# Opening of a graph layer kernel: rows of x and ids loaded first, weights behind the table rows, and part of the normalisation moved to GpSimd and VectorE

## The reference

```
gnn: e   = edge_attr @ W_edge + b_edge
     agg = segment_sum(relu(xn[src] + e), dst)
     h   = relu(((1 + eps) * xn + agg) @ W1 + b1) @ W2 + b2
     relu(batchnorm(h) * gamma + beta)
mix: linear attention over the nodes, 8 heads, weights Wq, Wkv, Wproj
ffn: softmax router, 8 experts, top 2 of them, two-layer MLP with gelu
```

## Time and profile before

| What | Value |
|---|---|
| Runs | 1181.65, 1177.09, 1177.69 us; median 1177.69 |
| Span of the profiled execution, first to last instruction | 1050.8 us |
| The profiled execution's own time | not given apart from its span; the median lies 126.9 us above the span |
| PE busy | 964.7 us (92%) |
| VectorE busy | 671.7 us (64%) |
| GpSimd busy | 555.1 us (53%) |
| ScalarE busy | 513.5 us (49%) |
| DMA | 198.30 MB, mean 189 GB/s |

### The profile page before, as it was taken

One profiled execution on the slowest core, in us unless ns is written; L12 is line 12 of the kernel. 1 busy time (PEld: TensorE's weight loads), 2 busy tenths in 40 slices (PEclk: granted clock), 3 DMA queues, 4 the chain that ended last, 5 costly groups with the idle time before them and its releaser, 6 DMA issues.

```text
span 1050.8 us, 17977 instructions
## 1 busy us (share of the span) xinstructions
PE 964.7 (92%) x5112; PEld 810.3 (77%) x5113; DVE 671.7 (64%) x1274; ACT 513.5 (49%) x1036; POOL 555.1 (53%) x627
## 2 busy tenths in 40 slices
PE   5898999999999999999998961799999999999994
PEld 4677888888888888877775860778888888888884
DVE  5455565656655565578886778666666666666663
ACT  3644555555454545455554566444444444444442
POOL 3277777777777777777760040224253353444442
PEclk8899999999999999999998986899999999999998
DMA  9667788788888878998762028412545636635321
GB/s 246 197 154 237 255 267 253 250 268 266 260 254 262 269 247 267 278 313 270 239 202 86 26 89 316 181 26 40 204 90 174 220 50 213 192 73 160 98 38 21
DMA packets 85472, 198.30 MB, mean 189 GB/s; under 512 B 19785, under 2 KB 37139, under 8 KB 84378
## 3 DMA queue, kind: packets, MB, share of 16 engines
q1 hardware_dynamic: 55926, 131.60, 36.1%
q0 software_dynamic: 28752, 64.45, 25.5%
q10 hardware_dynamic: 724, 1.42, 0.5%
HBM read 147.86 MB, written 49.97 MB: 188 GB/s over the span
## 4 chain that ended last, share of the span: by engine, by line
POOL 29%; PE 29%; DMA 19%; issue 13%; DVE 7%; ACT 2%; POOLq 1%; SPq 0%; DVEq 0%; ACTq 0%
POOL work L758 29%; DMA out<-work,rowc 11%; PE banks L1141 6%; PE banks L1166 4%; DMA work<-token_table,tokc 4%; PE banks L470 3%; PE banks L446 3%; PE banks L1168 2%; PE banks L969 2%; PE banks L1054 2%; PE banks L1151 2%; DMA work<-in_edge_attr 1%; PE banks L1042 1%; DMA wts<-in_src 1%; DVE st L1776 1%
## 5 line engine op out<-in xcount | busy, mean ns | idle before, releaser
L758 POOL DMA_INDIRECT work<-node_table,srcT x391 | 379.5, 971 | 157.0 <-issue 117.6
L470 PE MATMUL banks<-work 128*128 128x256 f32 x780 | 179.1, 379 | 1.1 <-issue 1.1
L446 PE MATMUL banks<-w_edge,eaT 128*128 128x256 f32 x780 | 179.3, 380 | 0.0
L470 PEld LDWEIGHTS banks<-work 128*128 128x128 f32 x780 | 148.0, 190 | 21.8 <-issue 1.8
L446 PEld LDWEIGHTS banks<-w_edge,eaT 128*128 128x128 f32 x780 | 143.4, 191 | 16.8
L1166 PE MATMUL banks<-wsplit,hidT_hi 128*128 x416 | 153.3, 408 | 2.1 <-DVE hidT_lo L1908 2.1
L529 DVE TENSOR_TENSOR work<-banks,work 128x512 f32<-128x512 f32 x195 | 126.8, 682 | 26.1 <-DMA work<-node_table,srcT 15.2
L1141 PE MATMUL banks<-wsplit,xeT_hi 128*128 x416 | 134.3, 404 | 2.8 <-DVE xeT_lo L1915 2.8
L483 ACT COPY wts<-banks 128x256 f32<-128x256 f32 x66 | 24.6, 372 | 228.8 <-PE banks L470 227.8
L811 POOL DMA_INDIRECT out<-work,rowc x52 | 83.4, 1605 | 82.2 <-ACT work L1441 45.6
L1168 PE MATMUL banks<-wsplit,hidT_lo 128*128 x416 | 116.8, 281 | 0.0
(11 more groups left out here) (263 smaller groups left out, 1555.2 us busy)
## 6 DMA issues: line engine op xcount, KB each, us to landing
wsplit<-split_table SPq DMA_DIRECT2D x8, 4096.0 KB, 15.3
work<-in_edge_attr SPq DMA_DIRECT2D x65, 384.0 KB, 4.6
wts<-in_L_ffn_W SPq DMA_DIRECT2D x64, 256.0 KB, 4.9
split_table<-raw_hi SPq DMA_DIRECT2D x64, 256.0 KB, 3.0
split_table<-raw_lo SPq DMA_DIRECT2D x64, 256.0 KB, 4.3
work<-node_table,srcT POOLq DMA_INDIRECT x391, 4.2
xs<-in_x SPq DMA_DIRECT2D x8, 560.0 KB
wts<-in_L_ffn_b SPq DMA_DIRECT2D x8, 512.0 KB, 4.0
```

Source lines behind the costliest of these rows:

```text
L446: last = nc.tensor.matmul(b[:, k * DIM:(k + 1) * DIM], eaT[:, u, 2 * q + k], w_edge[:], start=True, stop=True)
L470: last = nc.tensor.matmul(bank[5][:, 0:DIM], onehot[:, u, j], msg[:, u, j], start=(j == 0), stop=(j == GT - 1))
L758: pool.indirect_dma_start(out=xg[n % NB][0:rows, j], out_offset=None, in_=node_table, in_offset=bass.IndirectOffsetOnAxis(ap=srcT[0:rows, ...
```

## The change

Chunks 1 and 2 of x are now first on ScalarE's queue, ahead of the bias row, the router's weights, `eps` and `w_edge`; chunks 3 and 4 follow the ids on SP. The other weights are loaded behind the stores of the table rows. The rounds are (0), (1), (2), (3 and 4). The seven small steps from moments to variance run on POOL. The bias additions of chunks 0, 1, 2 run on POOL, those of 4 and 3 on VectorE, which also normalises chunk 4 itself. Every chunk has its own place in `table_stage`. The clearing of `hT` moves behind POOL's additions. The destination ids (`rel`) are worked out after the bias additions, and their transposes come after the routing. PE's transposes of x alternate between banks 0 to 2 and 3 to 5. The mixing weights are transposed in group 0 of the edge phase (`turn_weights`), in two halves with ScalarE's copies between them, and VectorE's first one-hot waits for them (`wT_ready` 2), since it shares their place in SBUF.

```diff
-STAGES = 4
-LEAD = ((0,), (1, 2), (3, 4))
+ROUNDS = ((0, 1), (1, 2), (2, 3), (3, 5))
+BY_POOL = 3
...
@@ sync @@
-            load_x(2)
+            load_x(3)
             load_x(4)
-            weights = [
...
-            for s, d in weights:
-                sp.dma_start(s, d).then_inc(weights_in, 16)
             load_edges(sp, 0, 0, 0, True)
-            load_edges(sp, 1, 1, 1, True)
...
+            for c, ready, n in ((0, rows_pool, 1), (1, rows_pool, 2), (4, rows_dve, 1), (2, rows_pool, 3), (3, rows_dve, 2)):
+                sp.wait_ge(ready, n)
+                for d, s in node_rows(node_table, table_stage[c], c):
+                    sp.dma_start(d, s).then_inc(rows_stored, 16)
+            sp.dma_start(w_natural[:, 2:6], a["L0_mix_Wkv"].rearrange("(r p) c -> p r c", p=P)).then_inc(weights_in, 16)
+            load_edges(sp, 1, 1, 1, True)
...
+            sp.wait_ge(rows_stored, 32 * CHUNKS)
@@ gpsimd @@
+            def moments(r):
+                lo, hi = ROUNDS[r]
+                pool.wait_ge(stats_ready, r + 1)
...
+                step(nc.gpsimd.tensor_tensor(L[:, 0], v[:, 1], v[:, 4], ALU.subtract))
+                step(nc.gpsimd.tensor_tensor(L[:, 1], v[:, 1], v[:, 4], ALU.add))
+                step(nc.gpsimd.tensor_tensor(L[:, 0], L[:, 0], L[:, 0], ALU.mult))
+                step(nc.gpsimd.tensor_tensor(L[:, 2], v[:, 2], v[:, 5], ALU.add))
+                step(nc.gpsimd.tensor_scalar(L[:, 2], L[:, 2], 1.0 / DIM, LN_EPS, ALU.mult, ALU.add))
+                step(nc.gpsimd.tensor_scalar(L[:, 0], L[:, 0], 0.25, None, ALU.mult))
+                step(nc.gpsimd.tensor_tensor(L[:, 2], L[:, 2], L[:, 0], ALU.add))
+                pool.sem_inc(var_ready, 1)
...
+            for r in range(3):
+                moments(r)
+            add_bias(0)
+            moments(3)
+            for c in range(1, BY_POOL):
+                add_bias(c)
             nc.gpsimd.memset(hT[:], 0.0).then_inc(h_zero, 1)
@@ tensor @@
+                if c == 1:
+                    pe.wait_ge(wc_ready, 1)
+                    pe.wait_ge(tables_ready, 2)
...
+            def turn_weights():
+                pe.wait_ge(weights_in, WEIGHT_DMAS * 16)
+                pe.wait_ge(miss_known, 1)
...
+                last.then_inc(wT_ready, 1)
+                pe.wait_ge(wT_copied, 2)
...
+                last.then_inc(wT_ready, 1)
+                pe.wait_ge(wT_copied, 4)
@@ vector @@
+            stats_of(0).then_inc(stats_ready, 1)
+            scale_of(0)
+            stats_of(1).then_inc(stats_ready, 1)
+            stats_of(2).then_inc(stats_ready, 1)
+            dve.wait_ge(ids_in, 64)
+            nc.vector.tensor_copy(src_f, src_i).then_inc(rel_ready, 1)
+            scale_of(1)
+            stats_of(3)
+            scale_of(2)
+            stats_of(4).then_inc(stats_ready, 1)
...
+            scale_of(3)
+            normalise_x(4)
+            dve.wait_ge(small_in, SMALL_DMAS * 16)
+            add_bias(4)
+            add_bias(3)
             dve.wait_ge(wc_sum, 1)
```

More of the change, by code:

```diff
@@ L134, in build @@
         onehot = view(work, 7680, 2, GT, P)
-        table_stage = view(work, 1536, STAGES * CHUNK_TILES, DIM).rearrange("p (u t) d -> p u t d", u=STAGES)
+        table_stage = [view(t, o, CHUNK_TILES, DIM) for t, o in ((work, 1536), (work, 2816), (work, 4096), (work, 5376), (wts, 0))]
         w_natural = view(work, 7168, 8, DIM)
@@ L283, in build @@
         xn_ready = sem("xn_ready")
-        rows_ready = sem("rows_ready")
-        rows_stored = [sem(f"rows_stored{i}") for i in range(STAGES)]
+        xn_last = sem("xn_last")
+        rows_pool = sem("rows_pool")
+        rows_dve = sem("rows_dve")
+        rows_stored = sem("rows_stored")
         ids_memset = sem("ids_memset")
@@ L874, in _ @@
             pe.wait_ge(rel_ready, 1)
-            nc.tensor.transpose(bank[6][0:1, 0:GROUPS], gstat[:, 0:1], ident[0:GROUPS, 0:GROUPS])
-            for j in range(GT):
-                nc.tensor.transpose(bank[4][:, j * GROUPS:(j + 1) * GROUPS], rel[:, j:GROUP:GT], ident[0:GROUPS, 0:GROUPS])
-            nc.tensor.transpose(bank[4][:, GT * GROUPS:(GT + 1) * GROUPS], rel[:, 0:P], ident[0:GROUPS, 0:GROUPS])
             for j in range(GT):
@@ L1212, in _ @@
         def _(act):
+            for c in (1, 2):
+                for d, s in node_rows(a["x"], xs[:, c * CHUNK_TILES:(c + 1) * CHUNK_TILES], c):
+                    act.dma_start(s, d).then_inc(x_in[c], 16)
             act.dma_start(b_edge[:], a["L0_gnn_b_edge"].partition_broadcast(P)).then_inc(small_in, 16)
@@ L1298, in copy_group, with copy_weights @@
                     copy_tail(act, n, n % 2)
+            def copy_weights():
+                act.wait_ge(wT_ready, 1)
+                for k in range(2):
+                    nc.scalar.copy(wkvT[:, k], bank[5 + k][:]).then_inc(wT_copied, 1)
+                act.wait_ge(wT_ready, 2)
+                for t, b in ((wqT, 5), (wpT, 6)):
+                    nc.scalar.copy(t[:], bank[b][:].rearrange("p (k c) -> p k c", k=2)).then_inc(wT_copied, 1)
             copy_group(0)
@@ L1493, in _, with stats_of, scale_of @@
             nc.vector.memset(src_i, 0).then_inc(ids_memset, 1)
-            def norm_of_x(r, chunks):
-                lo, n = chunks[0] * CHUNK_TILES, len(chunks) * CHUNK_TILES
-                for c in chunks:
-                    dve.wait_ge(x_in[c], 32)
-                    for t in range(c * CHUNK_TILES, (c + 1) * CHUNK_TILES):
-                        last = nc.vector.bn_stats(st[0:TILE, t], xs[0:TILE, t])
-                step(last)
-                moments_to_ln(step, lo, n)
-                dve.sem_inc(var_ready, 1)
+            def stats_of(c):
+                dve.wait_ge(x_in[c], 32)
+                for t in range(c * CHUNK_TILES, (c + 1) * CHUNK_TILES):
+                    last = nc.vector.bn_stats(st[0:TILE, t], xs[0:TILE, t])
+                return last
+            def scale_of(r):
+                lo, n = ROUNDS[r][0] * CHUNK_TILES, (ROUNDS[r][1] - ROUNDS[r][0]) * CHUNK_TILES
                 dve.wait_ge(sd_ready, r + 1)
@@ L1517, in _, with normalise_x @@
-            norm_of_x(0, LEAD[0])
+            def normalise_x(c):
+                dve.wait_ge(ln_ready, len(ROUNDS))
+                for t in range(c * CHUNK_TILES, (c + 1) * CHUNK_TILES):
+                    nc.vector.tensor_scalar(xs[0:TILE, t], xs[0:TILE, t], ln[0:TILE, 4, t:t + 1], ln[0:TILE, 5, t:t + 1],
+                                            ALU.mult, ALU.add).then_inc(xn_last, 1)
+            def add_bias(c):
+                if c < CHUNKS - 1:
+                    dve.wait_ge(xn_ready, CHUNK_TILES * (c + 1))
+                else:
+                    dve.wait_ge(xn_last, CHUNK_TILES)
+                nc.vector.tensor_tensor(table_stage[c][0:TILE], xs[0:TILE, c * CHUNK_TILES:(c + 1) * CHUNK_TILES],
+                                        b_edge[0:TILE].unsqueeze(1).to_broadcast([TILE, CHUNK_TILES, DIM]), ALU.add
+                                        ).then_inc(rows_dve, 1)
```

152 lines of the change are left out of this document (72 added, 80 removed).

## The result

The changed kernel took 1193.2 us (median of four runs, 1192.1 to 1196.1), the kernel before 1177.4 (1171.1 to 1181.7): 15.8 us more by the medians. By the ratio it is 1.0146 times as long, with a 95% interval of 1.0097 to 1.0195, or 17 us more. The forecast was 7.2 us more, at 1184.9 us, with a range up to 1190. The side and the mechanism were the likeliest case's; the size was missed by half, and one statement about the kernel before was wrong. The profiled execution took 1192.06 us, its span is 1190.3: 1.8 us lie around the span.

A forecast was written before the change was run, and what follows sets the result against it. PE was taken to set the pace from about 92 us. Sums of group 0 at 67.3 plus 31.6 gave 98.9 against 91.69, +7.2 us; on span 1050.8 plus 126.9, 1184.9 us (likeliest case, chance 0.50), range 1174 to 1190.

The forecast's parts named there:

- Bound and carrying: Edge phase: PE sets the pace from about 92 us, 7.585 us a group without idling; a later beginning carries through.
- the forecast's own sign of failure: Wrong as a whole if PE idles in the steady phase or its second transposition precedes the last bias addition.
- The median lies 126.9 above it, a part that the change does not touch: Whole program: median 1177.69 us against span 1050.8; the 126.9 us between them was added unchanged.
- The hold: Opening: VectorE's scale step and first normalisation wait for GpSimd's additions (25.2, 28.1), four normalisations for the memset (33.95).
- Ready routing columns at 38.4: Opening: VectorE finishes the routing columns, which PE's second transposition waits for, at 38.4 us, behind its last bias addition.
- 28.9 us from there to the end of the sums: From ready routing columns, PE's path through routing, embedding, weight turning and one-hot; sums of group 0 end at 67.3.
- embedding, top maximum and miss flag as one stretch, 3.3: First group, after routing and edge transpositions: these three steps together take 3.3 us.
- First gather 43.8, weights' DMAs nothing: Gathers start at 43.8 us as before; weights loaded behind the rows cost nothing, with 5 us to spare.
- VectorE keeps its turn: Opening: five normalisations pass in one run before the memset; +1.4 us, 1179.1 us, chance 0.18.
- no hold: Opening: GpSimd's additions do not hold VectorE, routing columns ready at 29.3; -1.9 us, 1175.8 us, chance 0.17.
- gathers decide: Edge phase: POOL, not PE, sets the pace, so earlier stored rows gain 10 us; 1168 us, chance 0.07.
- Worse: Opening: half clock lasts 2.5 us more, or moment steps cost 3.7 us more; 1191 us, chance 0.08.

The follow-up runs named there:

- before_again: The kernel before, run and profiled again unchanged; 1169.33 us in the profiled execution, ratio to before 1.0027.
- memset_early: The changed kernel with the memset of hT back ahead of the first moments on POOL; ratio to before 1.0130.
- adds_dve: The changed kernel with the bias additions of chunks 1 and 2 on VectorE instead of GpSimd; 1195.5 us, ratio to before 1.0182.
- all_three: The changed kernel with hT memset, routing columns, weight loads and kv turning earlier, PE's filler dropped, w_edge on its own semaphore; 1179.5 us.
- all_dve: all_three with the bias additions of all five chunks on VectorE and none on GpSimd; ratio to before 0.9980.
- raw_late: The changed kernel with the first three loads of expert weights held until edge group 3 is loaded; ratio to before 1.0207.
- after_small_stores: The changed kernel with stores of split expert weights cut to 16 of 128 partitions from expert 1 on; 1216.4 us, ratio to before 1.0213.

## Why the prediction was wrong

- **Bound and carrying.** That the place of the first groups is carried to the end held: group 2's gathers were 18.3 us later than in before_again, the sums of group 60 20.1 later (655.7 against 635.6), the median 15.8. That PE runs without a gap at 7.585 us a group did not: it holds only in the execution that was profiled first, and the forecast's own sign of failure (idle stretches of PE in the steady phase) is there. Over 48 groups PE idles 53 us in before_again and 62 in the changed kernel.
- **"The median lies 126.9 above it, a part that the change does not touch".** Wrong: the part around a span is 1.8 us. The sum itself was made of differences, so this moved no term, but it hid that the first profile lacked the late results and the half clock of the other executions.
- **The hold.** Right in kind: the scale step behind GpSimd's additions, the normalisations behind the memset. In detail it came otherwise. The last square root was given at 29.66 instead of 24.2, since ScalarE's copy of chunk 0's transposes stood ahead of it and PE made these at 27.20 only. So the scale step met the second addition and not the first, and all five normalisations lay behind the memset, not four. memset_early, adds_dve, all_three and all_dve show each part of it come and go.
- **Ready routing columns at 38.4.** Measured 42.2, 3.8 late. The memset started at 32.1 instead of 28.4, since the statistics began at 8.48 instead of 7.13, addition 0 waited for w_edge, which landed at 19.5 (its load took 15.2 us, and the forecast had no term for it), and GpSimd's additions held VectorE a first time (1.86 us from 20.64). So VectorE had measured chunk 4 at 24.15 instead of 20.7, which is most of the 3.7 us. The seven moment steps took 1.9 us instead of 1.75 (0.20 each, but 0.28 from start to start), an addition on GpSimd 2.9 instead of 2.69.
- **28.9 us from there to the end of the sums.** Measured 34.9. To the end of routing 18.3 against 19.7 forecast; the weights, one-hot and sums 6.2 against 5.9; but "embedding, top maximum and miss flag as one stretch, 3.3" took 10.4. **This is the step that failed most:** the forecast took it at full clock and without any wait. Of its 7.1 us too much, 1.9 are the half clock of the embedding (the forecast had its half clock earlier, in the routing), and 3.9 are PE's wait in front of group 1's transpositions (60.51 to 64.43), behind ScalarE's late copy at 63.49, and 1.3 are group 1's transpositions, which the forecast had counted into the time before. Why the copy was late stays open.
- The sum of the steps closes: 7.3 forecast for the gathers of group 2 (59.99 to 67.3), 3.8 and 6.0 from the two points above, 0.3 from the sums' end to the gathers, 0.9 since group 2's gathers stood at 59.1 and not 59.99 in a timed execution: 18.3.
- **First gather 43.8, weights' DMAs nothing.** The gather started at 49.2: 3.9 of the 5.4 us come from the last addition (it ended at 42.1 instead of 38.2), 1.5 from store and landing. The weights did land in time (the first turning waited 0.57 us for the miss flag, not for them), so their zero was right here.
- **The rivals.** VectorE keeps its turn, no hold, gathers decide: all excluded by the rows above. "Worse" had the right direction at 1191 and only its own two causes, of which neither was the one: that it came within 2 us of 1193 was luck.
- **The range** ended at 1190, 3 us short. It was made around one execution of a kernel whose executions spread by 19 us and more, and took in no case in which that execution was not like the others.

## What to carry to other kernels

If a profile's span and the median of the runs are far apart, don't put the difference outside the program: on this kernel 1.8 us lie outside and the rest inside, in one phase. When work is moved to GpSimd, look at what VectorE does at that moment and the other way round; additions on either engine stretched steps of 0.2 us on the other to between 1.5 and 2.8 us, and a memset of 5.5 us cost the normalisations 5.1. And where an order puts a gate (here two products for the routing) behind a queue of bulk work on one engine, move the gate first: of the single moves tried here it brought the most, 6 us by the ratios.

## What the runs showed of the hardware that I had not expected

- Results of PE reach ScalarE or VectorE after PE's recorded end: in the first groups by up to 8 us (5.1 in the changed kernel, 5.9 in all_dve, 7.0 in raw_late, 8.0 in after_small_stores, 1.8 in before_again, none at the same places in all_three or in the first profile), then by 0.7 to 1.6 us a group. Less bulk traffic didn't remove it, and the first profile, without it, moved more (260 GB/s from 100 to 150 us, against 191 in before_again); the granted clock was 1.00 from 50 to 62 us in the changed kernel, where it first appears. It lies between PE's record and PE's signal: in the changed kernel the semaphore's event for the product that ends at 58.40 stands at 63.47 in the trace, and ScalarE starts at 63.49. Whether PE's records run ahead of PE, or the signal comes late, no run here tells: **this stays open**, and with it why the first profile had none of it.
- The hold between VectorE and GpSimd goes both ways (2.80 us on GpSimd's step, 2.52 on VectorE's). The Trainium skill (SBUF — State Buffer, section "Who interferes with whom") has it so: whoever issues first keeps the shared pair of ports for the whole instruction, and tensor_scalar can be among those concerned. By that rule, the trace agrees: 6.84 us for five normalisations beside the memset, 1.70 without. The two directions are not quite alike: in all_three VectorE's step ended with the first of two additions in a row (29.14 and 29.11 us), in adds_dve GpSimd's step only with the second (26.98 and 26.89).
- The same kernel takes 1177 to 1179 us on two chips and 1194 to 1198 on two others. Only ratios on one chip can be compared.
